# Flamingo block with gated cross-attention: the steps of an attention round in another order on every engine

## Chip, core and metric

The program runs on one core of a Trainium2 chip. The metric is the device time of one execution in microseconds (us). TensorE is called PE here, VectorE DVE, ScalarE ACT, GpSimd POOL and SyncE SP, as in the profile.

## What is computed

A block of a Flamingo model in float32: cross-attention whose keys and values come from a context and from the latents themselves, and then a feed-forward part with a block-sparse choice of neurons. The change lies in the attention, so the reference is cut to it:

```python
# x: (4, 256, 512)  ctx: (4, 1601, 512)  32 query heads, 8 key/value heads, head size 128
kv = jnp.concatenate([context, latents], axis=1)          # 1857 rows a batch
q = (latents @ Wq); k = (kv @ Wk); v = (kv @ Wv)
q = rms_norm(q, q_norm_w); k = rms_norm(k, k_norm_w)
scores = jnp.einsum('bhgqd,bhkd->bhgqk', qg, k) * scale
probs = jax.nn.softmax(scores, axis=-1)
out = jnp.einsum('bhgqk,bhkd->bhgqd', probs, v)
return out @ Wo
```

## The kernel before

The program runs four parts one after the other: `prepare` (layer norm, Q projection), `attend`, `project` (times Wo) and `ffn`. The change touches `attend` alone, and in it the table of steps at L435 to L464.

**Rounds.** `attend` works in 32 rounds, one for each of 4 batches and 8 key/value heads. A round holds the four query heads of its group as 2 halves (h = 0 and 1) of 512 columns each, and the 1857 keys as 15 tiles (t) of 128 rows, the last of 65. Every product is made in three passes of high and low parts, so a step "qk" (scores of one tile) and a step "pv" (probabilities times V of one tile) are 3 matmuls each.

**Steps.** Each has a name, a half h and a tile t (or a group g of two tiles):
- On PE: `qk` (L653), `mt`/`mb` (transpose and spread of the column maxima, L660, L622), `pv` (L673), `dt`/`db` (the same for the denominators, L683, L622), `k` and `v` (projections of a chunk c of 512 keys in three parts a, b, c of 4 matmuls, L614; chunk 3 has 322 columns), `kn` (column sums of squares, L709), `vt` (V transposed, L723), `xt` (the context transposed, once a batch).
- On ACT: `copy` (scores out of PSUM, L745), `exp` (L750), `hi` (high part of the probabilities, L756), `oraw` (result out of PSUM, L760), `khi` (L766, L768), `vhi` (L773), `vthi` (L779).
- On DVE: `max` (L801), `red`, `sub` (minus the maximum, L812), `lo` (low part, L818), `dred`, `on`, `klo` (L834), `var` (L840), `vtlo` (L847).
- On POOL: `sum` (denominators, L864, L867), `fold` (L870), `pow` (key norms, L876, L878). On SP: the loads and stores.

Below, "qk 0.5" is half 0, tile 5; "sub 1.0" is half 1, group 0; "k 2a" is chunk 2, part a.

**Order.** Each step has a place, a number counted in tiles (15 to a half, 30 to a round). `steps.sort()` orders them, and every engine issues its own steps in that order; it never goes ahead of a step that waits. A place under 0 or from 30 on belongs to the round before or after, so a window of one round holds late steps of the last head, its own steps, and early steps of the next (FIRST, MIDDLE, LAST_LOADS, and BOUNDARY between two batches; START and TAIL at the ends). Scores of a half are all made first, and its exponentials and `pv` follow 24 tiles later, beside the `qk` of the next half: hence PE takes a `qk` and a `pv` by turns, with parts of `k` and `v` between them.

**Buffers that tie steps together.** `pqk` has 2 banks: `qk` of a tile waits for the `copy` of two tiles before. `pr` has NP = 2 groups: `hi` of a group waits for the last `pv` of the group two before. `ppv` has one bank: the first `pv` of a half waits for `oraw` of the last half. `pkv` has 2 banks, and the 16 uses of it in a round (`k`, `kn`, `v`, `vt` of four chunks) take them by turns in the order of the table; each waits (`wait_for_bank`) until what stood in its bank has been taken out: by `klo` after `k`, `var` after `kn`, `vhi` after `v`, `vtlo` after `vt`. The banks are dealt from MIDDLE at L510 to L512, so they follow the table.

## Time and profile before

| | us |
|---|---|
| median of 3 runs | 3681.51 (3675.87 to 3684.28) |
| profiled execution | 3666.57 |
| its span, first to last instruction | 3664.7 |
| attention, first `qk` to the last round's start | 299.0 to 3055.5 |

The profile gives busy time of each engine, and for each idle time of an engine what ended it ("<-" and the instruction that released it). PE's weight loads (PEld) run beside its matmuls. A matmul's shown duration is longer than its share of the pipeline, so what a step costs on PE is read from the start of one to the start of the next.

### The profile page before, as it was taken

To read this page: it belongs to the slowest core of one execution; us is meant where nothing else is said; L and a number is where in the kernel's file an instruction comes from. 1 tells how busy PE (TensorE), PEld (TensorE's weight loads), DVE (VectorE), ACT (ScalarE), POOL (GpSimd) and SP (SyncE) were. 2 spreads that over 40 slices of the span, in tenths; PEclk is the share of its full clock that TensorE was granted. 3 is DMA by queue.
4 is the path that set the end of the run, shared out by engine and by line. 5 is a ranking of instruction groups with operands and counts; after the bars stand their busy time and mean duration, and the time that the engine had idled before them with its cause. 6 is when DMAs were issued, how large, how long until landed. Compare 5 with 4: busy or idle time off the path is not lost. (4 is left out here: it accounts for less than half of the span.)

```text
span 3664.7 us, 52293 instructions
## 1 busy us (share of the span) xinstructions
PE 3162.6 (86%) x14906; PEld 2518.2 (69%) x14906; DVE 2476.6 (68%) x3316; ACT 2036.9 (56%) x2899; POOL 1343.4 (37%) x791
## 2 busy tenths in 40 slices
PE   7978888888888888888888888888888888599699
PEld 5856677767667677766677776767776777377477
DVE  6854767777857777777677777676777677632666
ACT  3435666666656666665566666666666666431211
POOL 2321444444524444444244444443444444400000
PEclk9989999999999999999999999999999999799799
DMA  7870000000210000102000100020100000243410
GB/s 241 262 232 30 30 29 29 29 29 29 68 39 29 29 29 31 34 23 80 24 29 31 34 29 29 23 79 27 35 29 29 29 29 18 81 149 97 148 35 18
DMA packets 183908, 210.88 MB, mean 58 GB/s; under 512 B 10964, under 2 KB 125652, under 8 KB 182760
## 3 DMA queue, kind: packets, MB, share of 16 engines
q1 hardware_dynamic: 179016, 196.27, 16.6%
q0 software_dynamic: 2176, 8.39, 0.7%
q10 hardware_dynamic: 2592, 4.72, 0.4%
q8 instruction: 59, 0.97, 0.1%
q14 instruction: 65, 0.53, 0.0%
HBM read 140.14 MB, written 69.21 MB: 57 GB/s over the span
## 5 line engine op out<-in xcount | busy, mean ns | idle before, releaser
L745 ACT ACTIVATE att_sc<-att_pqk,att_rk 128x512 f32<-128x512 f32 (+1 forms) x960 | 661.8, 689 | 865.6 <-PE att_pqk L653 844.2
L867 POOL TENSOR_TENSOR att_sm<-att_sm,att_sc 128x1024 f32<-128x1024 f32 (+1 forms) x384 | 849.4, 2212 | 754.3 <-DVE att_pr L818 753.3
L673 PE MATMUL att_ppv<-att_pr,att_V 128*128 128x512 f32 (+1 forms) x2880 | 896.0, 421 | 127.9 <-ACT att_oraw L760 85.4
L653 PE MATMUL att_pqk<-att_q,att_kT 128*128 128x512 f32 (+1 forms) x2880 | 855.0, 407 | 7.9 <-issue 5.9
L614 PE MATMUL att_pkv<-att_ctxT,att_wkv 128*128 128x512 f32 (+1 forms) x3072 | 772.0, 384 | 102.5 <-DVE att_V L847 102.3
L614 PEld LDWEIGHTS att_pkv<-att_ctxT,att_wkv 128*128 128x128 f32 x3072 | 565.2, 193 | 234.4 <-DVE att_V L847 113.0
L673 PEld LDWEIGHTS att_ppv<-att_pr,att_V 128*128 128x128 f32 (+1 forms) x2880 | 524.9, 196 | 259.9 <-ACT att_oraw L760 103.4
L818 DVE TENSOR_TENSOR att_pr<-att_sc,att_pr 128x1024 fp32r<-128x1024 f32 (+1 forms) x512 | 628.1, 1227 | 109.0 <-ACT att_pr L756 108.7
L801 DVE TENSOR_TENSOR att_pmx<-att_pmx,att_sc 128x512 f32<-128x512 f32 x768 | 533.0, 694 | 237.8 <-ACT att_sc L745 232.6
L653 PEld LDWEIGHTS att_pqk<-att_q,att_kT 128*128 128x128 f32 (+1 forms) x2880 | 542.0, 191 | 146.4 <-ACT att_sc L745 8.1
L812 DVE TENSOR_TENSOR att_sc<-att_sc,att_pmax 128x1024 f32<-128x1024 f32 (+1 forms) x512 | 584.6, 1142 | 0.0
L756 ACT CAST att_pr<-att_sc 128x1024 fp32r<-128x1024 f32 (+1 forms) x512 | 509.7, 996 | 87.1 <-PE att_ppv L673 86.3
L750 ACT ACTIVATE att_sc<-att_sc 128x1024 f32<-128x1024 f32 (+1 forms) x512 | 513.0, 1002 | 33.3 <-DVE att_sc L812 33.2
L876 POOL TENSOR_TENSOR att_rk<-att_var,att_mhalf 128x4 f32<-128x4 f32 (+1 forms) x128 | 137.8, 1077 | 507.9 <-DVE att_var L840 374.9
L864 POOL TENSOR_TENSOR att_sm<-att_sc 128x1024 f32<-128x1024 f32 x64 | 153.6, 2400 | 389.5 <-PE att_pred L683 243.6
L834 DVE TENSOR_TENSOR att_kT<-att_pkv,att_kT 128x512 fp32r<-128x512 f32 (+1 forms) x128 | 82.2, 642 | 233.8 <-ACT att_sq L768 233.8
L1020 PE MATMUL out_po<-out_wo,out_o 128*128 128x512 f32 x768 | 183.0, 401 | 29.6 <-DVE out_wo L996 23.6
L291 PE MATMUL pre_pq<-pre_wq,pre_xT 128*128 128x512 f32 x768 | 194.4, 403 | 6.0 <-issue 6.0
L1020 PEld LDWEIGHTS out_po<-out_wo,out_o 128*128 128x128 f32 x768 | 148.5, 194 | 64.0 <-issue 20.7
L709 PEld LDWEIGHTS att_pkv<-att_ones,att_sq 128*128 128x128 f32 (+1 forms) x960 | 120.5, 187 | 69.1 <-ACT att_vraw L773 58.1
L291 PEld LDWEIGHTS pre_pq<-pre_wq,pre_xT 128*128 128x128 f32 x768 | 141.0, 190 | 35.0 <-issue 6.4
L709 PE MATMUL att_pkv<-att_ones,att_sq 128*128 128x1 f32 (+1 forms) x960 | 114.5, 239 | 45.4 <-ACT att_vraw L773 44.1
(130 smaller groups left out, 2738.4 us busy)
## 6 DMA issues: line engine op xcount, KB each, us to landing
q_scr<-pre_qT SPq DMA_DIRECT2D x128, 256.0 KB, 3.6
att_wkv<-kv_scr SPq DMA_DIRECT2D x64, 512.0 KB, 4.1
att_q<-q_scr SPq DMA_DIRECT2D x64, 512.0 KB, 4.1
o_scr<-att_on SPq DMA_DIRECT2D x64, 256.0 KB, 2.0
out_oraw<-o_scr SPq DMA_DIRECT2D x64, 256.0 KB, 4.6
att_sc<-in_ctx SPq DMA_DIRECT2D x16, 768.0 KB, 4.7
pre_wq_raw<-in_L_xattn_Wq SPq DMA_DIRECT2D x8, 1024.0 KB, 7.0
kv_scr<-pre_kv SPq DMA_DIRECT2D x8, 1024.0 KB, 7.5
```

What stands on the lines that cost most here:

```text
L291: mm = pe.matmul(pq[:, t % 4], xT[:, xp, c, t * P:(t + 1) * P], wq[:, j, wp, c], start=(i == 0), stop=(i == 3 * KT - 1))
L614: mm = pe.matmul(bank, wkv[:, which, wp, t], ctxT[:, xp, t, a:z], start=(i == 0), stop=(i == len(terms) - 1))
L653: mm = pe.matmul(pqk[0:m, (h * NT + t) % 2], kT[:, kp, t * P:t * P + m], q[:, qp, h], start=(i == 0), stop=(i == 2))
L673: mm = pe.matmul(ppv[:], V[0:m, vp, t], pr[0:m, pp, (t // 2) % NP, t % 2], start=(t == 0 and i == 0), stop=(t == NT - 1 and i == 2))
L745: act.activation(sc[0:m, h, t], pqk[0:m, s % 2], ACT.Copy, scale=rk[0:m, t:t + 1]).then_inc(sc_ok, 1)
L750: act.activation(sc[0:m, h, i:i + z - a], sc[0:m, h, i:i + z - a], ACT.Exp).then_inc(exp_ok, z - a)
L756: act.copy(pr[0:m, HI, t % NP, 0:z - a], sc[0:m, h, i:i + z - a]).then_inc(phi_ok, z - a)
L801: dve.tensor_tensor(mx[:] if t == NT - 1 else pmx[:], sc[:, h, 0] if t == 1 else pmx[:], sc[:, h, t], ALU.max).then_inc(max_ok, 1)
L812: dve.tensor_tensor(sc[0:m, h, i:i + w], sc[0:m, h, i:i + w], pmax[0:m].unsqueeze(1).to_broadcast([m, w, HALF]), ALU.subtract).then_inc(su ...
L818: dve.tensor_tensor(pr[0:m, LO, t % NP, 0:w], sc[0:m, h, i:i + w], pr[0:m, HI, t % NP, 0:w].bitcast(F32), ALU.subtract).then_inc(plo_ok, w)
L867: pool.tensor_tensor(sm[0:m, 0:w], sm[0:m, 0:w], sc[0:m, h, i:i + w], ALU.add).then_inc(sum_ok, w)
L1020: mm = pe.matmul(po[:, t], o[:, v % SL, op, h], wo[:, wp, e * HC + h], start=(e == 0 and h == 0 and p == 0), stop=(e == NE - 1 and h == HC ...
```

## The change

The places of the table are given anew, and a place may now differ between the two halves and between chunks and parts. In a middle round each engine has as many steps as before (PE 100, ACT 76, DVE 78, POOL 20, SP 6), and each step is the same instruction with the same waits; only their order differs and, with it, which of the two `pkv` banks a use gets. The steps `k`, `v` and their evacuations move most: V of chunk 0 is now projected in the window of the round before, and `k` of chunk 3 wholly at the start of its own round. `pow 1` moves from the window before to the start of its round.

```diff
--- before.py
+++ after.py
@@ -433,34 +433,37 @@
 
 
         LAG = 24
-        steps = []
+        TILE = dict(copy=0.39, pv=24.5, sub=19.4, exp=21.0, hi=21.7, lo=22.4, sum=23.0, max=0.98)
+        END = dict(mt=(2.79, 0.69),
+                   red=(1.4, 0.7),
+                   mb=(5.2, 5.2),
+                   oraw=(23.4, 23.1),
+                   fold=(24.8, 23.1),
+                   dt=(24.67, 24.47),
+                   dred=(28.43, 26.63),
+                   db=(31.76, 40.56),
+                   on=(30.61, 30.51),
+                   st=(28.31, 28.31),
+                   ldq=(-29.9, -29.9))
+        CHUNK = (dict(k=(-12.68, -11.4, -10.76), v=(-1.68, -0.8, -0.46), khi=-10.76, klo=-10.23, kn=-6.46, var=-7.66, pow=-0.06, vhi=-1.36, vt=14.9, vthi=15.16, vtlo=15.24),
+                 dict(k=(-5.98, -5.2, -5.19), v=(6.6, 7.74, 8.52), khi=-3.46, klo=-3.13, kn=-0.16, var=0.44, pow=1.23, vhi=13.14, vt=16.8, vthi=17.26, vtlo=17.44),
+                 dict(k=(-4.21, -3.06, -2.67), v=(8.8, 13.12, 14.74), khi=-1.77, klo=-1.14, kn=3.64, var=2.73, pow=4.24, vhi=15.54, vt=21.9, vthi=21.06, vtlo=22.34),
+                 dict(k=(0.2, 0.24, 0.32), v=(20.0, 21.62, 22.64), khi=0.54, klo=1.17, kn=4.13, var=5.84, pow=6.54, vhi=22.24, vt=23.7, vthi=24.36, vtlo=24.54))
+        LOADS = dict(ldwk=-26.5, ldwv=-11.4)
+        steps = [(place, what, 0, 0) for what, place in LOADS.items()]
         for h in range(NH):
             for t in range(NT):
                 p = h * NT + t
-                steps += [(p, "qk", h, t), (p + 0.39, "copy", h, t), (p + LAG, "pv", h, t)]
+                steps += [(p, "qk", h, t), (p + TILE["copy"], "copy", h, t), (p + TILE["pv"], "pv", h, t)]
+                if t >= 1:
+                    steps += [(p + TILE["max"], "max", h, t)]
             for g, (t, z) in enumerate(GR):
-                p = h * NT + t + LAG
-                steps += [(p - 4.3, "sub", h, g), (p - 3.2, "exp", h, g), (p - 2.4, "hi", h, g), (p - 1.6, "lo", h, g)]
-                if g >= 1:
-                    steps += [(p - 0.9, "sum", h, g)]
-            for t in range(1, NT):
-                steps += [(h * NT + t + 1.18, "max", h, t)]
-            e = (h + 1) * NT
-            steps += [(e + 1.59, "mt", h, 0), (e + 1.7, "red", h, 0), (e + 3, "mb", h, 0)]
-            f = e + LAG
-            steps += [(f - 0.6, "oraw", h, 0), (f - 0.5, "fold", h, 0), (f + 1.17, "dt", h, 0), (f + 1.83, "dred", h, 0),
-                      (f + 3.76, "db", h, 0), (f + 4.21, "on", h, 0), (f + 4.31, "st", h, 0)]
-            steps += [(h * NT - NT + .1, "ldq", h, 0)]
-
-        for c, (k, v, vt) in enumerate(((-12.7, 1, 12.6), (-9, 6, 16.6), (-3.21, 13, 20.6), (-1.5, 17.5, 24.6))):
-            for i in range(PARTS):
-                steps += [(k + i * 0.82, "k", i, c), (v + i * 0.82, "v", i, c)]
-            k, v = k + (PARTS - 1) * 0.82, v + (PARTS - 1) * 0.82
-            steps += [(k + 0.9, "khi", 0, c), (k + 1.03, "klo", 0, c), (k + 3.5, "kn", 0, c),
-                      (k + 3.6, "var", 0, c), (k + 3.7, "pow", 0, c)]
-            steps += [(v + 0.9, "vhi", 0, c)]
-            steps += [(vt, "vt", 0, c), (vt + 0.76, "vthi", 0, c), (vt + 1.64, "vtlo", 0, c)]
-        steps += [(-28, "ldwk", 0, 0), (-10.4, "ldwv", 0, 0)]
+                p = h * NT + t
+                steps += [(p + TILE[what], what, h, g) for what in ("sub", "exp", "hi", "lo", "sum") if g >= 1 or what != "sum"]
+            steps += [((h + 1) * NT + place[h], what, h, 0) for what, place in END.items()]
+        for c, places in enumerate(CHUNK):
+            for what, place in places.items():
+                steps += [(p, what, i, c) for i, p in enumerate(place)] if what in ("k", "v") else [(place, what, 0, c)]
         steps.sort()
 
 
```

On PE, at the point where half 1 of the last round begins its `pv` (the row with L669, in the changed kernel L672, is the wait of `pv 1.0`). Before:

```order
L614 MATMUL att_pkv<-att_ctxT,att_wkv 128x512 x4
L667 REGISTER_ALU
L673 MATMUL att_ppv<-att_pr,att_V 128x512 x3
L651 REGISTER_ALU
L653 MATMUL att_pqk<-att_q,att_kT 128x512 x3
L667 REGISTER_ALU
L669 REGISTER_ALU
L673 MATMUL att_ppv<-att_pr,att_V 128x512 x3
```

Now:

```order
L676 MATMUL att_ppv<-att_pr,att_V 128x512 x3
L617 MATMUL att_pkv<-att_ctxT,att_wkv 128x512 x4
L636 REGISTER_ALU
L617 MATMUL att_pkv<-att_ctxT,att_wkv 128x512 x4
L654 REGISTER_ALU
L656 MATMUL att_pqk<-att_q,att_kT 128x512 x3
L670 REGISTER_ALU
L672 REGISTER_ALU
L676 MATMUL att_ppv<-att_pr,att_V 128x512 x3
```

Before, only `qk 0.8` stands between `pv 0.14` (third row) and `pv 1.0` (last row); now, with `pv 0.14` in the first row, `v 1c`, `v 2a` and `qk 0.9` do.

On PE, from `vt 1` (first row) on, in the second half of a round. Before:

```order
L723 MATMUL att_pkv<-att_ident,att_vraw 128x128 x4
L667 REGISTER_ALU
L673 MATMUL att_ppv<-att_pr,att_V 128x512 x3
L651 REGISTER_ALU
L653 MATMUL att_pqk<-att_q,att_kT 128x512 x3
L638 ISA
L614 MATMUL att_pkv<-att_ctxT,att_wkv 128x512 x4
L614 MATMUL att_pkv<-att_ctxT,att_wkv 128x322 x4
L667 REGISTER_ALU
L673 MATMUL att_ppv<-att_pr,att_V 128x512 x3
```

Now:

```order
L726 MATMUL att_pkv<-att_ident,att_vraw 128x128 x4
L654 REGISTER_ALU
L656 MATMUL att_pqk<-att_q,att_kT 128x512 x3
L641 ISA
L617 MATMUL att_pkv<-att_ctxT,att_wkv 128x512 x4
L670 REGISTER_ALU
L676 MATMUL att_ppv<-att_pr,att_V 128x512 x3
L660 ISA
L661 REGISTER_ALU
L663 MATMUL att_pred<-att_ident,att_mx 128x128 x4
```

Before, `v 3a` (the row of 322 columns) comes three steps after `vt 1`, whose bank it takes; now it stands 22 rows after `vt 1`, behind `qk 1.5`.

On POOL, from the start of a middle round: `sum` is L867 (now L870), `pow` L876 (now L879). Before:

```order
L866 REGISTER_ALU
L867 TENSOR_TENSOR att_sm<-att_sm,att_sc 128x1024
L873 ISA
L875 REGISTER_ALU
L876 TENSOR_TENSOR att_rk<-att_var,att_mhalf 128x4
L861 REGISTER_ALU
L867 TENSOR_TENSOR att_sm<-att_sm,att_sc 128x1024
L873 REGISTER_ALU
L875 REGISTER_ALU
L876 TENSOR_TENSOR att_rk<-att_var,att_mhalf 128x2
L878 TENSOR_TENSOR att_rk<-att_var,att_mhalf 65x1
```

Now:

```order
L869 REGISTER_ALU
L870 TENSOR_TENSOR att_sm<-att_sm,att_sc 128x1024
L876 ISA
L878 REGISTER_ALU
L879 TENSOR_TENSOR att_rk<-att_var,att_mhalf 128x4
L864 REGISTER_ALU
L870 TENSOR_TENSOR att_sm<-att_sm,att_sc 128x1024
L876 REGISTER_ALU
L878 REGISTER_ALU
L879 TENSOR_TENSOR att_rk<-att_var,att_mhalf 128x4
L864 REGISTER_ALU
L870 TENSOR_TENSOR att_sm<-att_sm,att_sc 128x1024
```

The first `sum` of the window (0.4) was followed by `pow 2`; now `pow 1`, `pow 2` and `pow 3` stand behind `sum` 0.4, 0.5 and 0.6.

## Rows read from the trace of the kernel before

**Rows 1.** The page: PE's busy time, and its granted clock in 40 slices.

```profile
PE 3162.6 (86%) x14906; PEld 2518.2 (69%) x14906; DVE 2476.6 (68%) x3316; ACT 2036.9 (56%) x2899; POOL 1343.4 (37%) x791
...
PEclk9989999999999999999999999999999999799799
```

**Rows 2.** Stretches: us, busy time by engine, granted PE clock, DMA share, GB/s.

```profile
299.00:361.50 62.50, 54.69 (x267) 43.00 (x265) 36.02 (x52) 36.06 (x57) 11.92 (x8) 1.00 0.08 26
361.50:881.40 519.90, 455.85 (x2216) 366.82 (x2214) 373.77 (x487) 338.91 (x481) 236.77 (x126) 0.98 0.09 30
1081.50:1598.20 516.70, 452.69 (x2215) 364.25 (x2214) 373.97 (x487) 338.87 (x481) 236.72 (x126) 0.99 0.09 31
1798.00:2328.80 530.80, 466.79 (x2215) 375.53 (x2215) 373.74 (x487) 338.92 (x481) 236.63 (x126) 0.96 0.09 30
2524.70:3055.50 530.80, 466.76 (x2216) 375.35 (x2215) 373.60 (x487) 338.80 (x481) 236.66 (x126) 0.96 0.09 30
625.40:710.80 85.40, 74.72 (x371) 60.10 (x370) 62.31 (x82) 56.53 (x81) 39.47 (x21) 1.00 0.09 31
1684.00:1734.00 50.00, 40.03 (x193) 30.64 (x191) 35.16 (x39) 26.48 (x37) 26.12 (x14) 0.91 0.12 44
```

**Rows 3.** Timeline of PE in the fifth round: start, us, instructions [idle before <-releaser].

```profile
635.19 1.16 PE L622 MATMUL att_pmax<-att_ident,att_red 128*128 128x128 f32 x8 [1.38 <-DVE att_sc L812]
...
639.13 0.72 PE L709 MATMUL att_pkv<-att_ones,att_sq 128*128 128x1 f32 x6 [1.39 <-ACT att_vraw L773]
...
651.22 0.97 PE L673 MATMUL att_ppv<-att_pr,att_V 128*128 128x512 f32 x3 [1.46 <-ACT att_oraw L760]
...
672.51 0.86 PE L614 MATMUL att_pkv<-att_ctxT,att_wkv 128*128 128x322 f32 x4 [2.07 <-DVE att_V L847]
...
682.63 0.66 PE L723 MATMUL att_pkv<-att_ident,att_vraw 128*128 128x128 f32 x4 [1.14 <-DVE att_kT L834]
...
692.55 0.97 PE L673 MATMUL att_ppv<-att_pr,att_V 128*128 128x512 f32 x3 [1.39 <-ACT att_oraw L760]
...
697.13 0.95 PE L673 MATMUL att_ppv<-att_pr,att_V 128*128 128x512 f32 x3 [0.47 <-DVE att_pr L818]
...
700.90 1.19 PE L614 MATMUL att_pkv<-att_ctxT,att_wkv 128*128 128x512 f32 x4 [1.34 <-DVE att_V L847]
```

**Rows 4.** The same timeline, a stretch of PE without idle time.

```profile
642.59 0.86 PE L673 MATMUL att_ppv<-att_pr,att_V 128*128 128x512 f32 x3
643.29 0.86 PE L653 MATMUL att_pqk<-att_q,att_kT 128*128 128x512 f32 x3
643.99 2.03 PE L614 MATMUL att_pkv<-att_ctxT,att_wkv 128*128 128x512 f32 x8
645.86 0.86 PE L673 MATMUL att_ppv<-att_pr,att_V 128*128 128x512 f32 x3
```

**Rows 5.** Groups of instructions in that round: busy us, mean ns | idle before.

```profile
L867 POOL TENSOR_TENSOR att_sm<-att_sm,att_sc 128x1024 f32<-128x1024 f32 (+1 forms) x12 | 26.6, 2214 | 23.2 <-DVE att_pr L818 23.2
L745 ACT ACTIVATE att_sc<-att_pqk,att_rk 128x512 f32<-128x512 f32 (+1 forms) x30 | 20.7, 689 | 25.6 <-PE att_pqk L653 25.4
L812 DVE TENSOR_TENSOR att_sc<-att_sc,att_pmax 128x1024 f32<-128x1024 f32 (+1 forms) x17 | 19.5, 1146 | 0.0
L818 DVE TENSOR_TENSOR att_pr<-att_sc,att_pr 128x1024 fp32r<-128x1024 f32 (+1 forms) x16 | 18.7, 1170 | 3.8 <-ACT att_pr L756 3.8
L876 POOL TENSOR_TENSOR att_rk<-att_var,att_mhalf 128x4 f32<-128x4 f32 (+1 forms) x4 | 4.2, 1056 | 10.7 <-DVE att_var L840 6.4 <-DVE att_var L842 4.3
```

**Rows 6.** Timelines of DVE, then of POOL, between two batches.

```profile
1709.30 2.57 DVE L818 TENSOR_TENSOR att_pr<-att_sc,att_pr 128x1024 fp32r<-128x1024 f32 x1
...
1720.12 2.74 DVE L818 TENSOR_TENSOR att_pr<-att_sc,att_pr 65x512 fp32r<-65x512 f32 x1
...
1708.38 2.41 POOL L867 TENSOR_TENSOR att_sm<-att_sm,att_sc 128x1024 f32<-128x1024 f32 x1 [1.38 <-DVE att_pr L818]
...
1719.95 2.36 POOL L867 TENSOR_TENSOR att_sm<-att_sm,att_sc 128x1024 f32<-128x1024 f32 x1
```

## The prediction, made before the changed kernel ran

> **What bounds the kernel now.** I read the page first. PE is busy 86% of the span and runs mostly at its full 2.4 GHz, while no other engine passes 68% [rows 1]. So time can be won only where PE idles or its clock is low. Next I cut attention into rounds. The 24 intervals between the starts of full rounds last 519.9 + 516.7 + 530.8 + 530.8 = 2098.2 us, or 87.4 each; the first rounds of the batches take about 63, since half the `pv` are missing, and the stretch between two batches takes 50 [rows 2]. The full rounds are the case.
>
> In one of them, 85.4 us long at full clock, PE is busy 74.7 us, DVE 62.3, ACT 56.5 and POOL 39.5 [rows 2]. PE idles in eight places, 1.38 + 1.39 + 1.46 + 2.07 + 1.14 + 1.39 + 0.47 + 1.34 = 10.64 us [rows 3], and the same eight come back in the other full rounds. The reader is to see in them that the releaser is an engine with time to spare each time: it is not too slow, but asked too late, or PE comes to the dependent step too soon.
>
> **What PE's steps cost.** From start to start, a `qk` or `pv` costs 0.70 us and a full part of `k` or `v` 0.93 [rows 4]; by the same reading of the round, a short part costs 0.60, `kn` 0.80, `mb` and `db` 0.87, a transpose 0.35 to 0.44. 60 x 0.70 + 18 x 0.93 + 6 x 0.60 + 4 x 0.80 + 4 x 0.87 + 8 small ones of 0.40 make 72 us. The round has 85.4, so its eight stalls cost 13.3, not 10.6: each also shows 0.33 of refilled pipeline. No step is added or taken away, so 72.1 us is the floor of a full round before and after.
>
> **The change, stall by stall.** I laid PE's new order out with these costs and followed the chains on the other engines, `copy` 0.69, `sub` 1.15, `lo` 1.2, `sum` 2.4, `pow` 1.06 [rows 5]. What matters is how much PE work now stands between the step that starts a chain and the step that waits for it.
> - `mb 1` waited for `sub 0.7`, which DVE had far back. It now stands after `qk 0.5` instead of before `pv 0.9`, 2.7 us of PE work later: gone.
> - `kn 3` waited for its bank, held by `v 0` until `vhi 0`, which ACT had behind `copy 0.3`. `v 0` has moved to the round before, and the bank's last user is now `k 3`, out about 3 us earlier: gone.
> - `pv 1.0` waited for `oraw` of the last half: after `pv 0.14` only `qk 0.8`, 0.70 us, against about 1 us of latency and queue and 0.58 of copy. Now `v 1c`, `v 2a` and `qk 0.9`, 2.6 us, stand there: gone. At `pv 0.0` it is the same, 0.70 us before and 3.1 now: gone.
> - `v 3a` waited for `vt 1`'s bank, 2.2 us of PE work for `vthi`, two steps in ACT's queue, and `vtlo`. Now about 8 us lie between: gone.
> - `vt 2` waited for `klo 0`, with 3.4 us of PE work behind the chunk. Now 5.6, against about 5.2 by my walk: gone, but with 0.4 to spare.
> - `pv 0.2` waited for `lo 0.1`. Now 2.3 us to spare.
> - `k 2a` waited for `vt 3`'s bank: 3.9 us before, 6.0 now, of which about 5.5 is needed.
>
> By this walk none of the eight stays; several new waits come within 0.4 to 0.6 us of it: `vt 2`, `kn 0`, `vt 3`, `k 2a`, and `pv 1.0` to `pv 1.4`, where DVE falls behind. A row error of half a microsecond turns each into a stall. The bound from below is 0; from above, five such places at 0.6 idle + 0.33 refill and one at 0.8 give 5.5. I take 3.0 us of stalls left in a round, a little over the middle, since waits come to light only when others have gone.
>
> The order of steps changes waits at one more place. `pow 1`, whose result `copy 0.4` reads, used to be done a round ahead; it now queues on POOL behind `sum 0.4`, which follows `lo 0.4`. By the walk it ends 1.7 us before `copy 0.4` needs it. `vhi 0` waits for `v 0c` at the head of ACT's queue, with `exp 0.4`, `copy 1.14` and `hi 0.4` behind it; PE has `kn 1`, `db`, `qk 0.0` and `k 3` meanwhile, and 1 to 2 us to spare. Both cost nothing as long as that cover is there. On SP, `ldwv` waits for `v 3c`, 15 us of PE work before `v 0a` needs the weights.
>
> **Clock.** Rounds without a low stretch take 85.4 us and the mean is 87.4, so the half clock costs 2.0 a round; in the second half of attention the granted clock is 0.96 against 0.98 to 0.99 [rows 2]. It falls after stretches in which PE has idled, and there will be fewer. Between 0 and 2.0, I leave 0.6.
>
> The Trainium skill (TensorE: Matmul & The Clock Gate, "HAM oscillation") says that idle gaps of PE drop the clock to half until it is busy again. The trace agrees in direction, 0.91 between batches where PE is busy 40 of 50 us against 0.96 and more in the rounds; the sum takes its cost from the rows alone.
>
> **The sum.** A full round: 72.1 + 3.0 + 0.6 = 75.7. There are 28 of them (24 intervals and the last of each batch, which takes about the same): 28 x (87.4 - 75.7) = 328 us less. The 4 first rounds have stalls of the same kinds without the `pv` ones; 63 becomes about 58: 20 less. The three stretches between batches run at the pace of DVE and POOL and not of PE; `mb 1` comes later there too, for which I take 2.5 each, 8 less. Start, tail, `prepare`, `project` and `ffn` stay. 3666.6 - 356 = 3311 for an execution like the profiled one. The median of the runs before lies 15 us over the profiled one, so 3325.
>
> **Rivals.**
> 1. Nearly all goes (chance 0.13): no new stall over 0.5 us a round and no low clock, 72.6 a round. 28 x 14.8 + 24 + 12 = 450 less: 3231.
> 2. DVE and POOL keep each other waiting (0.15). Between batches a `lo` took 2.57 us instead of 1.2 and the last, smaller one 2.74, and both times a `sum` was running on POOL; they ended 1.1 and 0.6 us after it [rows 6]. Two SBUF inputs and a POOL step thus take turns. In a round that is 39.5 us of POOL and 18.7 of `lo` [rows 2, 5], 58 of 72: no bound over the round. But where PE has only `qk` and `pv`, from `pv 1.0` to `qk 0.13`, it wants two tiles in 2.8 us, and `sum` with `lo` needs 3.6. Three pairs fall 2.5 us behind, at two such places in a round, on top of the 3.0: 28 x (87.4 - 80.7) + 27 = 215 less: 3466.
> 3. The other side (0.04 for slower): POOL's new order binds. If `sum 0.3` with `pow 0` and `sum 0.4` with `pow 1` (3.5 us each) always ran behind the two `lo` before them, ACT would stop at `copy 0.0` and `copy 0.4`, PE two tiles later, and `exp` and `hi` with ACT. Each us past the 1.7 to spare costs one a round. It decides against the change from 13.3 + 2.0 - 3.6 = about 12 us a round on. With each of two loops of `hi`, `lo`, `sum`, `pow`, `copy` (1.0 + 1.2 + 2.4 + 1.1 + 0.7 = 6.4 us) fully open to PE, 13 us: 3711. Against it speak the 1.7 us, and that POOL idles half the round.
> 4. The gain is not there (0.03): the stalls are set by something that the order does not touch, such as the latency of a semaphore, and move elsewhere: 3680.
>
> The Trainium skill (SBUF — State Buffer, "SBUF: two separate sides") says that a DVE operation with two SBUF inputs and a GpSimd operation that reads SBUF hold a shared port pair by turns, each for its whole length. The trace agrees [rows 6]; it would give rival 2, whose sum is made from the rows.
>
> **How the numbers follow.** The forecast, 3325, from about 3265 to 3395, has 0.65. The range for 8 in 10 takes in the forecast, half of rival 1 and half of rival 2: 3232 to 3455. A measurement of this kernel can tell about 0.2%, 7 us, from no change. Faster by more: 0.65 + 0.13 + 0.15 = 0.93, and 0.01 of rival 4. Within it: 0.02. Slower: 0.04.
>
> **What would show it.** Right: full rounds of 74 to 77 us; no idle time of PE before `v 3a`, `pv 1.0`, `pv 0.0` and `kn 3`; PE busy over 92% of a round. The clock row of attention should hold more 9s and the waits on `att_V`, `att_oraw` and `att_vraw` should go from the top of the list. Wrong: a `lo` of 2 us and more inside a full round, with PE waiting for `att_pr` (rival 2); PE waiting for `att_sc` at `qk 0.2` or `qk 0.6` and ACT for POOL's `att_rk` (rival 3); or eight stalls as before at other steps (rival 4).

## The result, and the profile after

The median of the changed kernel is 3213.0 us (4 runs, 3210.8 to 3223.4), beside 3680.6 of the kernel before in the same comparison: a ratio of 0.8736 with a 95% interval of 0.8714 to 0.8757, 468 us less. I had forecast 3325 with a range of 3232 to 3455. The direction was right, the size was not: the time lies 112 us below the forecast and 19 below the end of the range, close to what I had put down as rival 1 (3231, chance 0.13).

The profiled execution took 3211.7 us, its span is 3209.9. Lines of the changed kernel are 3 higher than before (`qk` L656, `pv` L676, `k` and `v` L617, `vt` L726, `mb` L625, `sub` L815, `lo` L821, `klo` L837, `vtlo` L850, `sum` L870, `pow` L879).

The page of after, busy time by engine and PE's granted clock in 40 slices [rows 1]:

```profile
PE 3026.6 (94%) x14906; PEld 2470.7 (77%) x14906; DVE 2455.7 (77%) x3316; ACT 2052.9 (64%) x2899; POOL 1317.7 (41%) x791
...
PEclk9998999999999999999999999999999998898899
```

The instructions are the same in number. PE is shown busy 136 us less: fewer of its matmuls run at the low clock, and a shown duration that reached into a stall now overlaps the next one. The 7s are gone from the clock row, and in attention nearly every slice is a 9.

Stretches of after, in the columns of [rows 2]: the first round, one of the four runs of six full rounds (the others give the same row to 0.05 us), the fifth round of attention alone, and 50 us between two batches.

```profile
298.00:353.90 55.90, 53.54 (x264) 42.61 (x263) 35.34 (x51) 34.78 (x55) 11.45 (x8) 1.00 0.11 37
353.90:788.40 434.50, 434.50 (x2216) 363.25 (x2216) 371.52 (x485) 342.33 (x482) 233.21 (x126) 1.00 0.10 35
571.10:643.50 72.40, 72.40 (x372) 60.53 (x370) 62.02 (x81) 56.91 (x82) 38.37 (x21) 1.00 0.11 36
1470.80:1520.80 50.00, 39.74 (x202) 31.12 (x200) 34.81 (x43) 28.86 (x40) 26.05 (x14) 0.97 0.18 64
```

The row of the fifth round says most: of 72.40 us PE is busy 72.40, at a granted clock of 1.00, which is 2.4 GHz. Six rounds take 434.5 us in every batch, where before they took 516.7 to 530.8. A full round of this kernel is now nothing but PE's own work, 72.4 us of it against the 72.1 that I had added up. In the 50 us between batches PE is busy as long as before (39.74 against 40.03): it still idles a fifth of the time there.

PE has no wait at all in that round. Of the other engines' waits (engine, line <- releaser: us in total, times, longest) the longest, and the longest for PE:

```profile
POOL att_sm L870 <- DVE att_pr L821: 23.3, 11, 4.6
...
ACT att_sc L748 <- PE att_pqk L656: 5.3, 9, 1.5
```

ACT waited 25.4 us for `qk` in a round before [rows 5] and waits 5.3 now: the other engines wait for PE less, since PE no longer waits for them.

**Where the 454.8 us of the span came from**, cut at the starts of rounds in both traces:

| | before | after | difference | forecast |
|---|---|---|---|---|
| up to the first `qk` | 299.0 | 298.0 | -1.0 | 0 |
| 24 full rounds | 2098.2 | 1738.0 | -360.2 | -280.8 |
| 4 first rounds | 253.1 | 223.5 | -29.6 | -20 |
| last round and stretch to the next batch, 3 times | 405.1 | 360.0 | -45.1 | } -54.8 |
| last round and tail | 125.4 | 111.1 | -14.3 | } |
| the rest | 483.9 | 479.3 | -4.6 | 0 |

The forecast's column is my sum cut the same way: 24 x 11.7; 20; and for both rows with a last round 4 x 11.7 + 8. Four fifths of the surprise, 79 of 99 us, are in these full rounds: 72.4 instead of 75.7.

### The profile page after: what moved, and what is told of

Its sections match the earlier page's. It is cut to its first block and busy times, and to the rows that moved or that the text cites. A ratio compares the mean times of both kernels' runs of the same rounds, so it can differ in the third digit from the quotient of the medians.

```text
span 3209.9 us, 52293 instructions
## 1 busy us (share of the span) xinstructions
PE 3026.6 (94%) x14906; PEld 2470.7 (77%) x14906; DVE 2455.7 (77%) x3316; ACT 2052.9 (64%) x2899; POOL 1317.7 (41%) x791
## 5 line engine op out<-in xcount | busy, mean ns | idle before, releaser
L870 POOL TENSOR_TENSOR att_sm<-att_sm,att_sc 128x1024 f32<-128x1024 f32 (+1 forms) x384 | 852.6, 2220 | 697.0 <-DVE att_pr L821 696.5
L676 PE MATMUL att_ppv<-att_pr,att_V 128*128 128x512 f32 (+1 forms) x2880 | 848.8, 404 | 22.8 <-DVE att_pr L821 20.1
L656 PE MATMUL att_pqk<-att_q,att_kT 128*128 128x512 f32 (+1 forms) x2880 | 850.1, 404 | 6.6 <-issue 3.8
L617 PE MATMUL att_pkv<-att_ctxT,att_wkv 128*128 128x512 f32 (+1 forms) x3072 | 756.3, 376 | 1.1 <-DVE att_kT L837 0.5
L821 DVE TENSOR_TENSOR att_pr<-att_sc,att_pr 128x1024 fp32r<-128x1024 f32 (+1 forms) x512 | 631.7, 1234 | 37.8 <-ACT att_pr L759 37.8
L617 PEld LDWEIGHTS att_pkv<-att_ctxT,att_wkv 128*128 128x128 f32 x3072 | 559.5, 189 | 120.6 <-DVE att_kT L837 1.2
L676 PEld LDWEIGHTS att_ppv<-att_pr,att_V 128*128 128x128 f32 (+1 forms) x2880 | 532.6, 191 | 149.3 <-DVE att_pr L821 35.1
L815 DVE TENSOR_TENSOR att_sc<-att_sc,att_pmax 128x1024 f32<-128x1024 f32 (+1 forms) x512 | 585.2, 1143 | 42.7 <-PE att_pmax L625 42.7
L656 PEld LDWEIGHTS att_pqk<-att_q,att_kT 128*128 128x128 f32 (+1 forms) x2880 | 505.8, 185 | 122.5 <-ACT att_sc L748 14.1
L867 POOL TENSOR_TENSOR att_sm<-att_sc 128x1024 f32<-128x1024 f32 x64 | 154.4, 2413 | 434.7 <-DVE att_pr L821 374.4
L879 POOL TENSOR_TENSOR att_rk<-att_var,att_mhalf 128x4 f32<-128x4 f32 (+1 forms) x128 | 129.6, 1012 | 92.4 <-DVE att_var L843 85.8
L237 POOL TENSOR_TENSOR pre_rq<-pre_ms,pre_mhalf 128x4 f32<-128x4 f32 x64 | 64.4, 1007 | 165.2 <-DVE pre_ms L349 165.2
L776 ACT COPY att_vraw<-att_pkv 128x512 f32<-128x512 f32 (+1 forms) x128 | 69.8, 545 | 90.8 <-PE att_pkv L617 90.8
```

The lines of the kernel that those rows point to most:

```text
L617: mm = pe.matmul(bank, wkv[:, which, wp, t], ctxT[:, xp, t, a:z], start=(i == 0), stop=(i == len(terms) - 1))
L656: mm = pe.matmul(pqk[0:m, (h * NT + t) % 2], kT[:, kp, t * P:t * P + m], q[:, qp, h], start=(i == 0), stop=(i == 2))
L676: mm = pe.matmul(ppv[:], V[0:m, vp, t], pr[0:m, pp, (t // 2) % NP, t % 2], start=(t == 0 and i == 0), stop=(t == NT - 1 and i == 2))
L815: dve.tensor_tensor(sc[0:m, h, i:i + w], sc[0:m, h, i:i + w], pmax[0:m].unsqueeze(1).to_broadcast([m, w, HALF]), ALU.subtract).then_inc(su ...
L821: dve.tensor_tensor(pr[0:m, LO, t % NP, 0:w], sc[0:m, h, i:i + w], pr[0:m, HI, t % NP, 0:w].bitcast(F32), ALU.subtract).then_inc(plo_ok, w)
L870: pool.tensor_tensor(sm[0:m, 0:w], sm[0:m, 0:w], sc[0:m, h, i:i + w], ALU.add).then_inc(sum_ok, w)
```

## What had to be explained

Three things. Are the eight stalls independent causes, each worth its own idle time, or does one feed another? Why did none of the new ones come that I had allowed 3.0 us for? And what does the clock do, which I had given 0.6 of 2.0 us? The theory of the prediction says: **stalls are local**. A round takes PE's work, and for each dependent step that PE reaches too soon the time by which it is too soon. The first rival says that **DVE and POOL** hold each other up on the SBUF port and that the order only hid it. The second says that **stalls shift or share a cause**: mend one, and the next waits longer. The third, that most of the gain is **the clock**. The expectations below number them in their own way: theory 1 is that stalls are local; theory 2, that spare time which the walk does not see takes a new stall in; theory 3, that a stall also brings the low clock; theory 4, that stalls shift or share a cause. DVE and POOL are called the rival of the prediction there.

Five experiments start from the changed kernel and put one thing back. Seven start from the kernel before and mend some of its stalls alone, by moving a few places in its table. Each ratio is against the kernel before in the same comparison, whose medians were 3676.2, 3684.6 and 3676.6 us.

## Putting one thing back into the changed kernel

**A short cover before `pv 1.0`.** `v 1c` and `v 2a` move ahead of `pv 0.14`, so that only `qk 0.9` stands between the end of one half's `pv` and the start of the next, as before the change.

```diff
-    dict(... v=(6.6, 7.74, 8.52), ...),
-    dict(... v=(8.8, 13.12, 14.74), ...),
+    dict(... v=(6.6, 7.74, 8.3), ...),
+    dict(... v=(8.4, 13.12, 14.74), ...),
```

> The changed kernel with v 1c and v 2a moved back ahead of pv 0.14, so that only qk 0.9 covers oraw before pv 1.0. Theory 1 (a stall costs its idle time plus 0.33 us of refill, and the walk from row durations is exact to 0.1 us): oraw starts 0.25 us after pv 0.14, takes 0.58, and pv 1.0 could start 0.70 after qk 0.9, so 0.4 us idle, 0.7 us a full round, 28 x 0.7 = 20 us more than the changed kernel (about 3233). Theory 2 (spare time that the walk does not see takes it in, which is why no new stall of those allowed for showed): 0 us. Theory 3 (a stall also brings the low clock back, up to 2 us a round): 40 us or more, and granted clock under 1.00 in full rounds.

Measured: 3226.6 us (ratio 0.878, 0.8733 to 0.8828), 14 more than the changed kernel, where theory 1 gave 20. The full rounds take 72.7 instead of 72.4, and none has a low clock. PE at that place, start and us:

```profile
592.84 0.86 PE L676 MATMUL att_ppv<-att_pr,att_V 65*128 65x512 f32 x3
593.54 0.86 PE L656 MATMUL att_pqk<-att_q,att_kT 128*128 128x512 f32 x3
594.45 0.96 PE L676 MATMUL att_ppv<-att_pr,att_V 128*128 128x512 f32 x3
```

`pv 1.0` starts 0.91 after `qk`, not 0.70: 0.21 late; the step behind it takes 0.11 longer, and the two are the 0.3 us of the round. In the kernel before, with the same 0.70 us of cover, `pv 1.0` starts at 651.22 [rows 3] behind this `qk`:

```profile
648.89 0.87 PE L653 MATMUL att_pqk<-att_q,att_kT 128*128 128x512 f32 x3
```

So there it is 1.63 late, of which 1.46 shows as idle. What differs is ACT. First the kernel before, then this run:

```profile
650.00 0.69 ACT L745 ACTIVATE att_sc<-att_pqk,att_rk 128x512 f32<-128x512 f32 x1 [0.62 <-PE att_pqk L653]
650.59 0.58 ACT L760 COPY att_oraw<-att_ppv 128x512 f32<-128x512 f32 x1
```

```profile
593.81 0.59 ACT L763 COPY att_oraw<-att_ppv 128x512 f32<-128x512 f32 x1 [1.06 <-PE att_ppv L676]
```

Before, `oraw` was queued behind the `copy` of the very `qk` that stood between the two `pv`; ACT had to wait for that `qk` first. In the changed table `oraw` is ahead of that `copy`, and starts when `pv 0.14` is through, 0.97 us after that one's start. Before, `pv 0.14` starts at 648.19 and `oraw` at 650.59, 1.43 later than by this measure. So of 1.63 us ACT's order was 1.4 and PE's cover 0.2. At `pv 0.0` the trace of before shows the same: `oraw` stands behind the `copy` of `qk 1.8` and starts 1.35 later than it could. This is read from the traces; no run moved `oraw` alone. I had seen the waits rightly and put the cause wholly on PE's order.

**`v 3a` early.** It takes the bank of `vt 1` and waits for `vtlo 1`. It goes back to shortly behind `vt 1`.

```diff
-    dict(k=(0.2, 0.24, 0.32), v=(20.0, 21.62, 22.64), ...)
+    dict(k=(0.2, 0.24, 0.32), v=(17.85, 21.62, 22.64), ...)
```

> The changed kernel with v 3a moved forward to stand right behind mt 0, before qk 1.3. Its bank comes free only with vtlo 1, which DVE ends 42.2 us into the round, while PE would reach v 3a at 38.9. Theory 1 (stall plus refill, nothing else): idle 3.4 us before v 3a, 3.7 us a round, 28 to 32 times: 104 to 118 us more than the changed kernel, granted clock 1.00 in full rounds. Theory 3 (long stalls are what brings the clock down): the same idle time, but low stretches of the clock in many rounds, and 130 to 170 us more. Theory 2 (spare time elsewhere gives part of it back): under 70 us more.

Measured: 3373.5 us (ratio 0.9189, 0.9138 to 0.924), 160 more, within what theory 3 gave and beyond theory 1. One number of the table gives back a third of the gain. PE in one full round:

```profile
708.00 1.44 PE L617 MATMUL att_pkv<-att_ctxT,att_wkv 128*128 128x322 f32 x4 [3.12 <-DVE att_V L850]
709.23 1.48 PE L656 MATMUL att_pqk<-att_q,att_kT 128*128 128x512 f32 x3
```

and the stretches ahead of, in and behind the stall, in the columns of [rows 2]:

```profile
697.00:704.00 7.00, 7.00 (x40) 5.96 (x39) 6.17 (x9) 6.51 (x10) 4.33 (x2) 1.00 0.07 26
704.00:707.10 3.10, 0.88 (x6) 0.50 (x4) 2.19 (x3) 0.77 (x1) 0.04 (x1) 1.00 0.63 195
707.10:713.90 6.80, 5.91 (x15) 4.86 (x16) 3.37 (x6) 1.73 (x2) 2.36 (x1) 0.50 0.00 0
713.90:720.00 6.10, 6.10 (x32) 5.13 (x31) 2.67 (x4) 4.15 (x7) 2.40 (x1) 0.99 0.00 0
```

PE has run 7 us without idle at clock 1.00, then idles 3.12 (704.88 to 708.00). 0.9 us before the end of this idle time the granted clock falls to 0.50, that is 1.2 GHz, and stays there for 6.8 us, though PE works again after the first 0.9 of them. A `qk` shown with 0.86 us at full clock takes 1.48 there. The full rounds come in three lengths: 75.8 in four of them, which have the stall and no low clock (3.4 more than 72.4), 77.3 and 78.5; the mean is 77.7. So of 5.3 us a round 3.4 are the stall and 1.9 the clock that it brings down, on average. One stall in the wrong place is dear by the two together.

**`vt 2` too soon, in two sizes.** In the changed kernel `klo 0` ends at 619.02 of the trace and `vt 2`, which needs it, starts at 619.60:

```profile
618.33 0.69 DVE L837 TENSOR_TENSOR att_kT<-att_pkv,att_kT 128x512 fp32r<-128x512 f32 x1
...
618.32 0.85 PE L676 MATMUL att_ppv<-att_pr,att_V 128*128 128x512 f32 x3
619.01 0.75 PE L617 MATMUL att_pkv<-att_ctxT,att_wkv 128*128 128x322 f32 x4
619.60 0.60 PE L726 MATMUL att_pkv<-att_ident,att_vraw 128*128 128x128 f32 x4
```

(the first line is DVE's, the others PE's). In the first run `vt 2` goes ahead of the 322-column part (0.60 us of PE work earlier), in the second ahead of a `pv` as well (1.30 earlier).

```diff
-    dict(... v=(8.8, 13.12, 14.74), ... vt=21.9, ...),
+    dict(... v=(8.8, 13.12, 14.74), ... vt=21.55, ...),   # the first run
+    dict(... v=(8.8, 13.12, 14.74), ... vt=21.4, ...),    # the second run
```

> The changed kernel with vt 2 moved ahead of v 3b alone, 0.6 us of PE work earlier, which is just the spare time that its trace shows there. Theory 1: klo 0 and vt 2 meet within 0.1 us, so 0 to 0.3 us a round, 0 to 10 us more than the changed kernel; against a_vt2_far this shows how sharp the edge of a stall is. The view behind the forecast (each wait within half a microsecond turns into a stall of 0.6 us idle and 0.33 refill): 0.9 us a round, 25 us more.

> The changed kernel with vt 2 moved ahead of pv 1.12 and v 3b, 1.3 us of PE work earlier. In the changed kernel klo 0 frees its bank 0.6 us before vt 2 starts. Theory 1: 0.7 us idle and 0.33 refill, 1.0 us in each of 28 rounds and about 1.3 in the 4 first ones: 30 to 35 us more than the changed kernel. Theory 2 (hidden spare time): under 10 us more. Theory 3 (clock too): over 60 us more.

Measured: 3216.1 us (ratio 0.8751, 0.8703 to 0.8799) and 3232.1 (0.8796, 0.8748 to 0.8843), 3 and 19 more than the changed kernel; rounds of 72.5 and 73.2. The places, near and then far:

```profile
618.89 0.86 PE L676 MATMUL att_ppv<-att_pr,att_V 128*128 128x512 f32 x3
619.64 0.66 PE L726 MATMUL att_pkv<-att_ident,att_vraw 128*128 128x128 f32 x4
```

```profile
622.32 0.86 PE L656 MATMUL att_pqk<-att_q,att_kT 128*128 128x512 f32 x3
623.77 0.66 PE L726 MATMUL att_pkv<-att_ident,att_vraw 128*128 128x128 f32 x4 [0.59 <-DVE att_kT L837]
...
623.03 0.68 DVE L837 TENSOR_TENSOR att_kT<-att_pkv,att_kT 128x512 fp32r<-128x512 f32 x1
```

`klo 0` ends at 623.71 in the far run and `vt 2` starts 0.06 later. So in the changed kernel it could have started at 619.08 and had 0.52 to spare. From that: 0.60 earlier should be 0.08 late, 1.30 earlier 0.78 late. In the near run `vt 2` starts 0.75 behind the `pv` instead of 0.70, so 0.05 late; in the far run 1.45 behind the `qk` instead of 0.70, so 0.75 late. The edge is sharp to a twentieth of a microsecond, and behind it a round pays the lateness about one for one (72.4 + 0.75 = 73.2). No full round of either run has a low clock.

The near run came as theory 1 had it. The far run's size was a miss, 19 us against the 30 to 35 that I had expected, since I had added 0.33 of refill to an idle time of 0.7 which already was the whole lateness. Of the 0.75 late, 0.59 shows as idle; half of what I had called "0.33 of refilled pipeline" is this difference, since a matmul's shown duration is longer than its share of the pipeline.

**POOL relieved.** Every `sum` but the first of a half adds only 64 of its 512 columns; the rest of the denominators is left out. PE, ACT and DVE do all they did.

```diff
-    pool.tensor_tensor(sm[0:m, 0:w], sm[0:m, 0:w], sc[0:m, h, i:i + w], ALU.add)
+    pool.tensor_tensor(sm[0:m, 0:w, 0:64], sm[0:m, 0:w, 0:64], sc[0:m, h, i:i + w, 0:64], ALU.add)
```

> The changed kernel with every sum on POOL but the first of a half adding 64 of its 512 columns alone (the rest of the denominators is left out). Theory 1 (PE bounds full rounds; lo and sum take turns but that is hidden): full rounds stay at 72.4 us; only the stretches between batches and the tail get shorter, by about 2 to 5 us each, 8 to 20 us in all. The rival of the prediction (DVE and POOL hold each other up in full rounds) would show a lo of 1.2 us everywhere and shorter full rounds; with PE never idle there, that cannot be.

Measured: 3203.3 us (ratio 0.8704, 0.8676 to 0.8731), 10 less than the changed kernel, whose interval overlaps, and within the 8 to 20 that theory 1 gave to the stretches outside full rounds. The round of 72.4 is unchanged to the tenth while POOL is busy 17 us in it instead of 38. The round, and its groups of `sum` and `lo` (busy us, mean ns of one), then `lo` in the changed kernel:

```profile
573.40:645.80 72.40, 72.40 (x371) 60.53 (x370) 61.23 (x81) 56.92 (x82) 17.05 (x21) 1.00 0.11 36
...
L870 POOL TENSOR_TENSOR att_sm<-att_sm,att_sc 128x128 f32<-128x128 f32 (+1 forms) x12 | 5.2, 437 | 40.4 <-DVE att_pr L821 40.4
...
L821 DVE TENSOR_TENSOR att_pr<-att_sc,att_pr 128x1024 fp32r<-128x1024 f32 (+1 forms) x16 | 18.4, 1152 | 1.3 <-ACT att_pr L759 1.3
```

```profile
L821 DVE TENSOR_TENSOR att_pr<-att_sc,att_pr 128x1024 fp32r<-128x1024 f32 (+1 forms) x16 | 19.4, 1213 | 1.0 <-ACT att_pr L759 1.0
```

`lo` is 0.06 us shorter without the long sums, 1 us a round in all, and PE does not see it. This ends rival 2 for the full rounds of the changed kernel: the two engines do hold each other up, but PE never waits for it.

## Mending single stalls of the kernel before

In these seven a few places of the old table move and nothing else. `VP` and `KP` stand for new places of parts of `v` and `k`. The lines of the traces are up to 2 higher than before.

**`mb 1` alone.** It goes to where the changed kernel has it.

```diff
-            steps += [(e + 1.59, "mt", h, 0), (e + 1.7, "red", h, 0), (e + 3, "mb", h, 0)]
+            steps += [(e + 1.59, "mt", h, 0), (e + 1.7, "red", h, 0), (e + (3, 5.2)[h], "mb", h, 0)]
```

> The kernel before with mb 1 alone moved, from before pv 0.9 to after qk 0.5, as in the changed kernel. Theory 1 (stalls add): 1.38 + 0.3 us off each of 28 full rounds, 48 us less than before. Theory 4 (a late release further on takes the time back, since DVE and ACT are not earlier than before): the stall goes, but kn 3 or v 3a waits longer, under 25 us less.

Measured: 3615.1 us (ratio 0.9842, 0.98 to 0.9884), 61 less than before, where theory 1 gave 48. One full round of it, all its idle times of PE over 0.3 us:

```profile
626.91 0.72 PE L709 MATMUL att_pkv<-att_ones,att_sq 128*128 128x1 f32 x6 [1.39 <-ACT att_vraw L773]
...
639.90 1.55 PE L673 MATMUL att_ppv<-att_pr,att_V 128*128 128x512 f32 x3 [1.46 <-ACT att_oraw L760]
...
662.73 0.86 PE L614 MATMUL att_pkv<-att_ctxT,att_wkv 128*128 128x322 f32 x4 [2.07 <-DVE att_V L847]
...
674.43 0.66 PE L723 MATMUL att_pkv<-att_ident,att_vraw 128*128 128x128 f32 x4 [1.13 <-DVE att_kT L834]
...
684.36 0.95 PE L673 MATMUL att_ppv<-att_pr,att_V 128*128 128x512 f32 x3 [1.39 <-ACT att_oraw L760]
...
688.93 0.96 PE L673 MATMUL att_ppv<-att_pr,att_V 128*128 128x512 f32 x3 [0.48 <-DVE att_pr L818]
...
692.70 1.19 PE L614 MATMUL att_pkv<-att_ctxT,att_wkv 128*128 128x512 f32 x4 [1.33 <-DVE att_V L847]
```

Beside [rows 3]: the first one is gone and the other seven stand there to 0.01 us. This stall did not feed the others. Yet the full rounds fell from 87.4 to 86.3 on average, not by the 1.7 that the stall was worth (1.38 + 0.33), so that the 24 of them brought 28 us and not 41. The stretches between batches, last round included, gave another 17.5 (387.6 for the three instead of 405.1): `mb 1` had waited there too, 3.86 us each time. So the total came out above 48 us for a reason that theory 1 had not counted.

**`vhi 0` earlier on ACT**, by 0.35 places, ahead of a `copy`. It frees the bank for `kn 3`.

```diff
-            steps += [(v + 0.9, "vhi", 0, c)]
+            steps += [(v + 0.9 + {0: -0.35}.get(c, 0), "vhi", 0, c)]
```

> The kernel before with vhi 0 on ACT moved ahead of copy 0.3, one step earlier; nothing moves on PE. Theory 1: kn 3 finds its bank free, 1.39 + 0.3 us off each of 28 full rounds and of the 4 first ones, 54 us less than before. Theory 4: DVE and PE only reach their next meeting earlier, v 3a waits longer by part of it, under 25 us less.

Measured: 3605.1 us (ratio 0.9806, 0.9764 to 0.9848), 71 less, where theory 1 gave 54. `kn 3`'s stall is gone, the other seven stand at 1.38, 1.46, 2.07, 1.13, 1.39, 0.48 and 1.34. One step on an engine that is busy two thirds of the time was worth 2% of the kernel.

**Both of these.**

> The kernel before with both one-place repairs at the start of a round, mb 1 and vhi 0. Theory 1: 3.4 us off a full round, 102 us less than before. Theory 4: idle time before v 3a, pv 1.0 or vt 2 grows; the sum of the single runs is not reached, or the two together give more than the sum because DVE, which idles 4.85 us for kn 3 at this place, gets ahead for the rest of the round and with it shortens the wait before v 3a: then 120 us or more.

Measured: 3568.0 us (ratio 0.9716, 0.9673 to 0.9759), 109 less, where theory 1 gave 102; idle 7.85 a round, the six others unchanged. Two of its rounds:

```profile
615.10:700.60 85.50, 77.59 (x371) 62.67 (x369) 63.21 (x82) 56.70 (x81) 39.65 (x21) 0.96 0.09 31
1058.90:1141.20 82.30, 74.37 (x370) 60.15 (x369) 62.80 (x82) 56.54 (x81) 39.66 (x21) 1.00 0.10 33
```

The same steps, the same idle time (85.50 - 77.59 = 7.91; 82.30 - 74.37 = 7.93), and 3.2 us apart: PE's busy time is longer by that at a granted clock of 0.96.

**`v 3a` later**, with its other parts and `vhi 3`.

```diff
+            VP, KP = {(0, 3): 18.9, (1, 3): 19.4, (2, 3): 20.1}, {}
...
-            steps += [(v + 0.9, "vhi", 0, c)]
+            steps += [(v + 0.9 + {3: 0.96}.get(c, 0), "vhi", 0, c)]
```

> The kernel before with the three parts of v 3 moved later by one to two steps each, so that 3.9 us more of PE work lie between vt 1 and v 3a, and vhi 3 later to suit. Theory 1: 2.07 + 0.3 us off each of 28 full rounds and 1.5 + 0.3 off the four first ones, 73 us less than before. Theory 4: vt 2, which follows, waits longer by what v 3a no longer does; under 35 us less.

Measured: 3625.5 us (ratio 0.9852, 0.9815 to 0.9889), 59 less, where theory 1 gave 73. The 2.07 before `v 3a` are gone, and `vt 2` waits 0.54 instead of 1.14. But `mb 0`, which had a part of `v 3` ahead of it, now comes too soon for `sub 1.7`, the last one that reads what `mb 0` overwrites:

```profile
664.57 2.06 PE L623 MATMUL att_pmax<-att_ident,att_red 128*128 128x128 f32 x8 [1.96 <-DVE att_sc L813]
```

Idle in all is 9.94, only 0.70 less than before. That isn't a stall that feeds another: the PE work that I moved away was the cover of `mb 0`.

**The `oraw` pair.** `v 1b`, `v 1c` and `k 1c` move later, to stand between the last `pv` of one half and the first of the next, and `khi 1`, `klo 1`, `vhi 1` and `kn 0` follow them.

```diff
+            VP, KP = {(1, 1): 8.2, (2, 1): 8.6}, {(2, 1): -6.8}
...
+            late = 0.76 * (c == 1)
+            steps += [(k + 0.9 + late, "khi", 0, c), (k + 1.03 + late, "klo", 0, c), (k + 3.5 + 0.66 * (c == 0), "kn", 0, c),
...
+            steps += [(v + 0.9 + {1: 0.96}.get(c, 0), "vhi", 0, c)]
```

> The kernel before with only the two oraw stalls covered: v 1b and v 1c stand between qk 0.8 and pv 1.0, kn 0 and k 1c between qk 1.8 and pv 0.0, and vhi 1, khi 1 and klo 1 a little later to suit. Theory 1 (stalls add up, each idle time plus 0.3 us of refill): 1.46 + 1.39 + 0.6 = 3.4 us off each of 28 full rounds, 97 us less than before, and some more if the clock falls less often. Theory 4 (the stalls hang together; PE arrives earlier at the next late release and waits there instead): the two are gone but vt 2, vt 3, v 3a or mb 1 wait longer, and under 50 us less.

Measured: 3611.8 us (ratio 0.9817, 0.9783 to 0.9851), 73 less, where theory 1 gave 97. `pv 1.0`, `pv 0.0` and `pv 0.2` no longer wait and `k 2a` waits 0.81 instead of 1.34, but `vt 3` now waits 2.00 for the `klo 1` that I had moved:

```profile
687.99 0.55 PE L725 MATMUL att_pkv<-att_ident,att_vraw 128*128 128x128 f32 x3 [2.00 <-DVE att_kT L836]
```

**The last two together**, and then **all four repairs**.

> The kernel before with both repairs at once. Theory 1: their sum, 170 us less than before, 5.8 us less a full round, so 79.5 us for a round at full clock, five stalls left. Theory 4: less than either theory-1 sum; the sum of b_oraw and b_v3a is not reached. For the clock: if it is the number of stalls in a stretch that brings it down, the granted clock of full rounds goes to 0.99 or more and the gain exceeds the sum.

> The kernel before with all repairs so far at once: mb 1, vhi 0, both oraw covers and v 3 later. Left as before: vt 2, vt 3 and k 2a. Theory 1 in its plain form: 7.8 us of the 10.6 us idle a round go, with refill 9.2 us, 28 x 9.2 = 258 us less than before, and the clock at 1.00 on top. Theory 4: each repair shows the next late release (b_both already showed mb 0 at 1.97 and vt 3 at 2.00); with four more gone, 3 to 5 us a round stay idle and low clock stretches with them, so 150 to 220 us less.

Measured: 3582.8 us (ratio 0.9735, 0.9704 to 0.9765), 102 less, against 59 and 73 for its halves and the 170 expected; and 3425.5 us (0.9318, 0.9274 to 0.9362), 251 less, where theory 1 gave 258 and theory 4 at most 220. All four together bring more than the sum of their pairs, 109 and 102. PE's idle times in a full round with all four:

```profile
641.50 1.16 PE L624 MATMUL att_pmax<-att_ident,att_red 128*128 128x128 f32 x8 [1.97 <-DVE att_sc L814]
...
650.35 0.66 PE L725 MATMUL att_pkv<-att_ident,att_vraw 128*128 128x128 f32 x4 [0.53 <-DVE att_kT L836]
...
662.40 0.55 PE L725 MATMUL att_pkv<-att_ident,att_vraw 128*128 128x128 f32 x3 [2.00 <-DVE att_kT L836]
...
667.77 1.20 PE L616 MATMUL att_pkv<-att_ctxT,att_wkv 128*128 128x512 f32 x4 [0.81 <-DVE att_V L849]
```

The idle times are those of the single runs (1.96, 0.54, 2.00, 0.81) to a hundredth. Over all these runs the idle time adds up: `v 3a` took 0.70 of it away and the `oraw` pair 1.86, both 2.57; `mb 1` with `vhi 0` 2.79, all four 5.33. The three runs fell short of what I had expected by the new waits of `mb 0` and `vt 3`, and the pair by its low clock besides (2.7 us a round, in the table below). What does not add up shows in two rounds of the kernel with all four:

```profile
598.50:677.60 79.10, 73.77 (x370) 60.21 (x369) 62.13 (x82) 56.30 (x81) 40.94 (x21) 1.00 0.10 33
1020.40:1102.60 82.20, 76.89 (x370) 62.82 (x369) 62.15 (x82) 56.28 (x81) 40.93 (x21) 0.96 0.10 33
```

**All kernels by one rule.** Work is 72.1 + idle + 0.33 for each stall, the length of a full round at full clock. The last column is the mean of the 24 full rounds less the round without a low stretch (the shortest where it has none, else the worked-out one). The 0.33 was fitted to the kernel before; the other rows test it.

| | stalls, idle | worked out | shortest | mean | low clock costs |
|---|---|---|---|---|---|
| before | 8, 10.64 | 85.4 | 85.3 | 87.4 | 2.1 |
| `v 3a` later | 8, 9.94 | 84.7 | 84.7 | 86.5 | 1.9 |
| `mb 1` | 7, 9.26 | 83.7 | 85.2 | 86.3 | 2.6 |
| `vhi 0` | 7, 9.25 | 83.7 | 85.3 | 85.5 | 1.9 |
| `oraw` pair | 6, 8.78 | 82.9 | 83.1 | 85.2 | 2.1 |
| `oraw` pair, `v 3a` | 6, 8.07 | 82.1 | 83.6 | 84.8 | 2.7 |
| `mb 1`, `vhi 0` | 6, 7.85 | 81.9 | 82.3 | 85.0 | 2.7 |
| all four | 4, 5.31 | 78.7 | 79.1 | 79.9 | 0.8 |
| changed, `v 3a` early | 1, 3.12 | 75.6 | 75.8 | 77.7 | 1.9 |
| changed, `vt 2` far | 1, 0.59 | 73.0 | 73.2 | 73.2 | 0 |
| changed | 0, 0 | 72.1 | 72.4 | 72.4 | 0 |

The left half adds up within 0.4 us; in the three kernels where the shortest round lies 1.5 above the worked-out one, every round has a low stretch. The right half does not add up: a round of the same kernel is the one without plus 1, 2 or, in two rounds, 3 times about 1.6 us (85.3, 86.9, 88.5, 90.0 before; 82.3, 83.9, 85.5 with `mb 1` and `vhi 0`; 79.1, 80.7, 82.2 with all four). Taking away up to a quarter of the idle time left this price about as it was or made it larger; taking away half of it more than halved the price, and without idle time it is nothing. I looked at where they begin: all low stretches in the full rounds of these kernels begin within about 2 us behind the end of an idle time of 1.3 us or more, or during it (up to 1.1 us before the end of the 3.12, up to 0.2 before the end of one of 2.0), and none has one of 0.8 or less as the last idle time ahead of it. With all four repairs there are 12 in 24 rounds, each behind one of the two idle times of 1.97 and 2.00. Why of two rounds with the same idle times one has such a stretch and the next has not, the runs do not show. Their place drifts by 0.1 us or so against the round from one round to the next (with `vhi 0` they begin 47.1, 47.0, 46.9, 46.8 us after the starts of four successive rounds), as if they kept a time of their own; that is a hint and no more.

So the low clock, 2.1 us a round before, did not come back with the first quarter of the idle time; 1.3 of it came with half of the idle time gone, and the rest with the last. Of the 15.0 us that a round lost, 12.9 were stalls and 2.1 the clock that they cost: theory 3, most of the gain, is refuted, but the stalls alone do not give the time either.

## Why the prediction missed

- **"None of the eight stays": right.** PE does not idle once in a full round. For six of the eight, `mb 1`, `kn 3`, `v 3a`, `vt 2` and both `oraw` waits, a run took the wait away or put it back by the cause named; `pv 0.2` and `k 2a` were never tried alone. For the two `oraw` waits the share of PE's cover was too high, since ACT's order carried 1.4 of 1.6 us.
- **"72.1 us is the floor": right**, 72.4 measured.
- **"I take 3.0 us of stalls left in a round": the step that failed.** It is 0.3 at most. 28 x 2.7 = 76 us of the 99 us by which the profiled execution lies under my 3311. I took the middle between no new stall and six, as if nothing were known, though my own walk said none, with 0.4 to 0.6 to spare. That is the mistake: an allowance with no particular wait behind it. The places that I had named do have spare time in the traces of the changed kernel: 0.3 us at `kn 0`, 0.5 at `vt 2` (I had 0.4), 0.8 at `k 2a` (0.5), 0.9 at `vt 3`, 1.0 at `pv 1.0` for `oraw` and 1.5 or more from there to `pv 1.4` for `lo`; and `pow 1` ends 3.0 us before `copy 0.4` starts (1.7). The nearest of them, `kn 0`, waits for `vhi 3`: that ends at 623.06 in one round, and `kn 0` starts at 623.41, where it could have started at 623.11. A small part of the difference comes from reading the steps of DVE and ACT as shown durations and not from start to start: a `copy` of 0.69 us is followed after 0.59, a `lo` of 1.2 after 1.14, while my 1.15 for `sub` was near the 1.13 measured. The near and far runs of `vt 2` show that an error of half a microsecond could have made a stall there or not: its edge lies within 0.05 us. That all of these places hold is thus shown by the run; the walk alone made it likely.
- **"Between 0 and 2.0, I leave 0.6" of the clock: 0.6 too much**, 17 us. It follows from the first miss: in the full rounds without a stall the clock never fell.
- **First rounds**: 55.9 rather than 58, 8 us, for the same reason.
- **Between batches**: 8 forecast. Cut in the traces at the first step of PE behind the last round, the three stretches lost 3.9 us together and the tail another 3.7; the four last rounds themselves lost 51.7. With `mb 1` moved alone the three stretches had lost 10.8, so other waits took most of that back: PE idles there for DVE and for the transfers of the next context. Low stretches of the clock, which last 34 us in these three before and 27 after, blur a difference of this size.
- **The 15 us from profiled execution to median**: the median of after lies 1.3 above its profiled execution, so this was 13 us too much. Executions of before reach from 3652.6 to 3690.8 in these comparisons and those of after from 3210.8 to 3223.4. The former scatter with the clock: of the 20 executions of before in these comparisons the fastest (3652.6 us) has the highest mean granted clock, 0.958, and the slowest (3690.0 and 3690.8) have 0.949 and 0.950; over all 20, 0.001 less of it goes with about 3.5 us more (correlation -0.92). That is what more or fewer low stretches would do; the profiled execution of before, at 0.955, had fewer than most.
- **Rival 1** was the case, 3231 against 3213 measured, and deserved the greater chance: my walk was an argument for it, and against it stood only caution. It adds 12 us for the stretches between batches, of which 4 came, and 0.5 us of stalls a round, of which at most 0.3 did.
- **Rival 2** is refuted for the full rounds of the changed kernel by the run with narrow sums. `lo` beside POOL's work does take longer, 1.72 us for `lo 1.0` beside a `fold` and 1.45 and 1.37 for `lo 1.2` and `lo 1.3`, but `pv 1.0` starts 1.8 us after that `lo` ends and no `pv` behind it waits:

```profile
589.26 1.72 DVE L821 TENSOR_TENSOR att_pr<-att_sc,att_pr 128x1024 fp32r<-128x1024 f32 x1 [0.66 <-ACT att_pr L759]
...
588.61 1.29 POOL L873 TENSOR_TENSOR att_sm<-att_sm 128x512 f32<-128x512 f32 x1
```

  On the shared port the trace agrees with the Trainium skill (SBUF — State Buffer, "SBUF: two separate sides"): this `lo` ends 1.1 us after the `fold` beside it. It cost nothing here, since no one waited for what was late.
- **Rival 3** did not come: `pow 1` starts at 576.94, at once behind its `sum`, and ends at 577.94; `copy 0.4` starts at 581.00.
